# Projections of queries and keys multiplied into the convolutions' weights on chip

## The chip, the cores and the metric

The kernel runs on one core of one Trainium2 chip. The metric is the device time of one execution in microseconds. TensorE (PE), VectorE (DVE), ScalarE (ACT), GpSimd (POOL) and SyncE (SP, which here issues all DMAs) run their own instruction lists in order and meet at semaphores.

## What is computed

A decoder layer on x of 8 batches by 128 positions by 128 features, float32: attention with convolutions, attention over a context, and a mixture of experts, each on a normalised x and added to x. The change concerns the queries and keys of the first attention:

```python
q_in = linear(x, Wq_w, Wq_b).transpose(0, 2, 1)
Q3 = conv1d(q_in, convq_w, convq_b, (1, 1))
Q_cat = jnp.concatenate([q_in, Q3], axis=1).transpose(0, 2, 1)
Q = linear(Q_cat, qproj_w, qproj_b).reshape(b_, l_, H, DK).transpose(0, 2, 1, 3)
...
tau = sigmoid(conv1d(gelu(conv1d(x_conv, tau1_w, tau1_b, (1, 1), groups=D)), tau2_w, tau2_b, (0, 0)))
delta = sigmoid(conv1d(gelu(conv1d(x_conv, del1_w, del1_b, (1, 1), groups=D)), del2_w, del2_b, (0, 0)))
scores = jnp.einsum('bhqd,bhkd->bhqk', Q, K) / sqrt(DK)
scores = scores * tau[..., None] + delta[:, :, None, :]
```

Keys are made as queries are, with weights of their own. The convolutions have three taps and zero padding of one position at either end of each batch. H is 16, DK 8.

## The kernel before, in words

The features lie on the 128 partitions, the 1024 positions (8 batches of 128) along the free axis. A PSUM bank holds 512 float32 columns, so work goes in two halves c of four batches. Matrix products go through the helper `mm` (L473), so the profile gives nearly all of them line 474; they are told apart by their operands.

*Start.* SP loads x (L346), the first constants up to `kpb` (L348, semaphore `ld_f`), the rest of them (L349, `ld_a`), the context, `pack_b`, the mask and expert weights. VectorE makes the mean and variance, then the normalised `xn`, one batch at a time (L294). TensorE meanwhile folds the second projection into the convolution's three taps (L490 to L494: three 128x128 products for queries, three for keys, and a one-column product for each bias). VectorE copies the folds out of PSUM and adds the first projection to the middle tap (L1131 to L1136): `foldq`, `foldk`, `foldb`.

*Turned x.* TensorE turns the eight batches (L478), ScalarE copies each half into `xnT` (L875), which has a zero column at either end of each batch.

*Queries and keys.* TensorE multiplies `xnT` by `wqT` and `wkT` (L501 to L505, four 512-column products), ScalarE adds the biases and writes `qin` and `kin` (`biased`, L894), and TensorE runs three shifted products per half on these with the folded weights (L509 to L524).

*Taps.* The depthwise convolutions of tau and delta: ScalarE makes the first tap of each of four blocks (`first_tap`, L888), VectorE adds two more (`later_taps`, L1138), ScalarE takes gelu (L922, L926). TensorE sums tau's two blocks to one row per head (L516), ScalarE takes the sigmoid (L929), VectorE multiplies it onto the queries (`qc`, L1178).

*High and low parts.* Queries and keys are split into a float32r high part (ScalarE, `high_keys` L902, `high_queries` L933) and the remainder (VectorE, `low_keys` L1189, `low_queries` L1183). TensorE stacks them per group of heads with the selection matrices `pick` (L541 to L558), which waits for the high and low keys of both halves. ScalarE fills rows of the stacks with constants (L882), and SP copies these over for the second attention's keys (`get_maxima`, L376). SP then stores the split rows (L410 to L414) and loads the per-step key blocks (L427).

Then follow 16 steps of attention and 66 units of experts, which the change does not touch.

The order on every engine is written out by hand. PSUM banks: 2 and 3 hold the folds, 4 the folded biases, 0 and 1 the turned x, 5 and 6 the queries, 7 and 0 the keys, 3 and 4 tau.

Of the kernel before, what the change touches and what calls it, by code (L numbers as in the profile page):

```python
# [11 lines left out]
ALU = mybir.AluOpType  # L12
# [3 lines left out]
P = 128  # L16
B = 8
T = B * P
H, DK = 16, 8
G = 4  # L20
# [41 lines left out]
def decoder_layer(nc, x, ctxT, mask, pack_a, pack_b, w3, rowsd, outT):  # L62
# [3 lines left out]
    with ExitStack() as ctx:  # L66
# [32 lines left out]
        foldq = oT[:, 0:3, :]  # L99
# [30 lines left out]
        foldk = early[:, 0:3 * P].rearrange("p (k o) -> p k o", k=3)  # L130
# [59 lines left out]
        in_done = sem("in_done")  # L190
        in_copied = sem("in_copied")
# [277 lines left out]
        def _(pe):  # L469
# [20 lines left out]
            for n, (conv_w, proj, bias) in enumerate((("cq", "qp2T", "cqb"), ("ck", "kp2T", "ckb"))):  # L490
                for k in range(3):
                    c0 = cols_a[conv_w][0] + P * k
                    mm(bank[2 + n][:, P * k:P * k + P], pa[:, c0:c0 + P], A(proj))
                mm(bank[4][:, n:n + 1], A(proj), A(bias)).then_inc(folded, 1)  # L494
            for c in range(2):
                turn_inputs(0, c, bank[c])
            pe.wait_ge(ld_a, 16)
            pe.wait_ge(ld_ctx, 16)
            pe.wait_ge(ld_b, 16)
            pe.wait_ge(pads_ready, 6)  # L500
            for c in range(2):  # L501
                pe.wait_ge(xT_copied, c + 1)
                mm(bank[5 + c][:, :], A("wqT"), half(xnT, c)).then_inc(in_done, 1)
            for c in range(2):
                mm(bank[7 - 7 * c][:, :], A("wkT"), half(xnT, c)).then_inc(in_done, 1)  # L505

            pe.wait_ge(fold_copied, 4)
            pe.wait_ge(in_copied, 2)
            for c in range(2):  # L509
                for k in range(3):  # L510
                    last = mm(bank[5 + c][:, :], foldq[:, k, :], half(qin, c, k), k == 0, k == 2)
                last.then_inc(q_done, 1)

            pe.wait_ge(gelu_done, 2)
            pe.wait_ge(const_ready, 1)
            for c in range(2):  # L516
                for r in range(2):
                    last = mm(bank[3 + c][:, :], tau2r[:, r, :, :], conv[:, r, 4 * c:4 * c + 4, :], r == 0, r == 1)
                last.then_inc(tau_done, 1)
            pe.wait_ge(in_copied, 4)  # L520
            for c in range(2):
                for k in range(3):
                    last = mm(bank[7 - 7 * c][:, :], foldk[:, k, :], half(kin, c, k), k == 0, k == 2)
                last.then_inc(k_done, 1)  # L524

# [340 lines left out]
        def _(act):  # L866
# [10 lines left out]
            act.wait_ge(pads_ready, 6)  # L877
# [3 lines left out]
            for g in range(G):  # L881
                act.activation(kst[0][:, g, 4:B, :].rearrange("p b t -> p (b t)"),  # L882
                               xnT[:, 0, 0:1].broadcast_to([P, HALF]), ACT.Identity,
                               bias=key_rows[:, g:g + 1]).then_inc(kst_filled, 1)
            copy_inputs(0, 0, 0)
            copy_inputs(0, 1, 1)
# [6 lines left out]

            def biased(dst, n, bias, banks):  # L894

                for c in range(2):
                    act.wait_ge(in_done, 2 * n + c + 1)
                    act.activation(half(dst, c, 1), four(banks[c]), ACT.Identity, bias=A(bias)).then_inc(in_copied, 1)
# [16 lines left out]
            biased(qin, 0, "bq", (5, 6))  # L915
            first_tap(0, 1, "tau1", "tau1b")
            first_tap(1, 0, "del1", "del1b")
            biased(kin, 1, "bk", (7, 0))
            first_tap(1, 1, "del1", "del1b")
            for r in range(2):  # L920
                act.wait_ge(conv_done, r + 1)
                act.activation(conv[:, r, :, :], conv[:, r, :, :], ACT.Gelu).then_inc(gelu_done, 1)  # L922
            for r in range(2):
# [10 lines left out]

            act.wait_ge(k_done, 1)
            act.wait_ge(fold_copied, 4)
            high_keys(0, 0, 7, foldb[:, 1:2])
            high_queries(0)
            act.wait_ge(k_done, 2)
            high_keys(0, 1, 0, foldb[:, 1:2])  # L940
            high_queries(1)
# [164 lines left out]
        def _(dve):  # L1106
# [24 lines left out]
            for n, (dst, proj) in enumerate(((foldq, "qp1T"), (foldk, "kp1T"))):  # L1131
                dve.wait_ge(folded, n + 1)
                link(dve.tensor_copy(dst[:, :, :].rearrange("p k o -> p (k o)"), bank[2 + n][:, 0:3 * P]))
                dve.tensor_tensor(dst[:, 1, :], dst[:, 1, :], A(proj), ALU.add).then_inc(fold_copied, 1)
            for n, bias in enumerate(("qpb", "kpb")):
                dve.tensor_tensor(foldb[:, n:n + 1], bank[4][:, n:n + 1], A(bias), ALU.add).then_inc(fold_copied, 1)  # L1136
# [16 lines left out]
            for at in range(3):  # L1153
                for m in (Q_PARTS[at], 2 + K_PARTS[at]):
                    rows = pick[:, m, :, :].rearrange("p g r -> p (g r)").rearrange("p (h r) -> p h r", h=H)
                    dve.wait_ge(rows_ready, 3)
                    last = dve.tensor_copy(rows[:, :, S_MAX:32].rearrange("p h (d a) -> p h a d", a=3)[:, :, at, :],
                                           ident.rearrange("p (h d) -> p h d", h=H))
            last.then_inc(picks_ready, 1)
# [33 lines left out]
            dve.wait_ge(fold_copied, 4)  # L1193
# [648 lines left out]
```

## Time and profile before

| | us |
|---|---|
| median of 3 runs | 303.61 (303.39 to 304.05) |
| the profiled execution | 304.08 |
| its span, first to last instruction | 302.3 |
| PE busy | 284.5 (94%) |
| DVE busy | 228.2 (76%) |
| ACT busy | 192.6 (64%) |
| POOL busy | 184.0 (61%) |

TensorE is busy nearly all of the span, but busy shares are means over stages. A float32 matrix product is two MATMUL records with a weight load (LDWEIGHTS, PEld) each; one of float32r is a single record. Times within the trace count from the first instruction.

### The profile page before, as it was taken

How to read it: one execution, taken by the hardware profiler on the slowest of the kernel's cores; microseconds unless marked ns; L12 is line 12 of the kernel's file. 1: busy time of each engine (PE TensorE's matmuls, PEld its weight loads, DVE VectorE, ACT ScalarE, POOL GpSimd, SP SyncE). 2: the span in 40 equal slices, each digit the busy share in tenths (PEclk: the TensorE clock that was granted, in tenths of full speed). 3: DMA queues.
4: the chain of work that ended last, by engine and by line, in shares of the span. 5: the costliest groups of instructions: out<-in, count | busy, mean ns of one | idle time of the engine just before them, and what ended most of it. 6: DMA issues, size and time to landing. Idle time of an engine off the chain costs nothing.

```text
span 302.3 us, 5347 instructions
## 1 busy us (share of the span) xinstructions
PE 284.5 (94%) x1675; PEld 203.1 (67%) x1675; DVE 228.2 (76%) x512; ACT 192.6 (64%) x352; POOL 184.0 (61%) x262
## 2 busy tenths in 40 slices
PE   1999999999999999899889999999999999999994
PEld 1734576666655565456665788888888888888883
DVE  3896798799859886987896559789956676676664
ACT  2797747796884566456742797766655555555552
POOL 8240062097708870985177799999975665665661
PEclk9999989999999999999999999999999999999999
DMA  7920535457577243350000637666333353344321
GB/s 260 266 44 1 192 71 150 105 125 254 102 187 136 64 104 98 87 132 10 2 1 25 203 107 223 198 200 188 129 102 137 105 173 128 124 133 134 119 62 37
DMA packets 30636, 37.18 MB, mean 123 GB/s; under 512 B 5136, under 2 KB 19856, under 8 KB 30608
## 3 DMA queue, kind: packets, MB, share of 16 engines
q1 hardware_dynamic: 30608, 36.84, 42.2%
q8 instruction: 14, 0.23, 0.4%
q14 instruction: 14, 0.11, 0.1%
HBM read 28.43 MB, written 3.93 MB: 107 GB/s over the span
## 4 chain that ended last, share of the span: by engine, by line
PE 83%; DVE 9%; ACT 4%; DMA 2%; issue 2%; SPq 0%; ACTq 0%; DVEq 0%
PE bank L474 57%; PE bank L813 5%; PE bank L815 5%; PE bank L814 5%; PE bank L619 2%; PE bank L594 2%; PE bank L637 2%; DMA pa<-pack_a 2%; DVE rawmax L1214 2%; PE bank L606 1%; PE bank L480 1%; ACT conv L891 1%; PE bank L642 1%; PE bank L603 1%; ACT conv L922 1%
## 5 line engine op out<-in xcount | busy, mean ns | idle before, releaser
L1779 POOL TENSOR_TENSOR qbd<-vs,qbd 128x512 fp32r<-128x512 f32 x65 | 83.7, 1291 | 33.3 <-ACT qbd L1093 33.3
L474 PE MATMUL bank<-khl,stacks 128*128 128x512 f32 x396 | 101.4, 392 | 1.9 <-DVE vs L1575 1.9
L474 PEld LDWEIGHTS bank<-khl,stacks 128*128 128x128 f32 x396 | 73.6, 188 | 18.6 <-issue 3.7
L1606 DVE TENSOR_TENSOR conv<-bank,conv 128x512 f32<-128x512 f32 x60 | 41.5, 691 | 31.4 <-ACT bank L1057 28.3
L1057 ACT ACTIVATE bank<-bank 128x512 f32<-128x512 f32 x61 | 35.5, 582 | 43.9 <-PE bank L474 43.9
L1214 DVE TENSOR_REDUCE rawmax<-bank 128x4 f32<-128x512 f32 x64 | 43.3, 684 | 9.4 <-PE bank L474 8.4
L1093 ACT ACTIVATE qbd<-vs 128x512 fp32r<-128x512 f32 x65 | 40.6, 625 | 7.1 <-DVE vs L1583 4.6
L1614 DVE TENSOR_TENSOR vs<-conv,bank 128x512 f32<-128x512 f32 x61 | 41.9, 687 | 2.1
L474 PE MATMUL bank<-stacks 128*128 128x512 f32 x96 | 41.5, 482 | 1.1 <-DVE stacks L1524 0.6
L981 ACT ACTIVATE conv<-bank 128x512 f32<-128x512 f32 x64 | 35.1, 597 | 6.4 <-PE bank L474 5.6
L1743 POOL TENSOR_TENSOR stacks<-ring,stacks 128x384 fp32r<-128x384 f32 x33 | 33.7, 1021 | 1.4
L474 PE MATMUL bank<-qbd,stacks 128*128 128x512 f32 x64 | 30.3, 520 | 0.6 <-ACT conv L981 0.6
L990 ACT ACTIVATE qbd<-bank 32x512 fp32r<-32x512 f32 x40 | 23.4, 586 | 10.7 <-PE bank L606 10.4
L813 PE MATMUL bank<-qbd,stacks 128*128 128x512 f32 (+1 forms) x67 | 26.4, 394 | 0.7 <-POOL qbd L1779 0.6
L815 PE MATMUL bank<-qbd,stacks 128*128 128x512 f32 (+1 forms) x67 | 25.9, 387 | 0.0
L814 PE MATMUL bank<-qbd,stacks 128*128 128x512 f32 (+1 forms) x67 | 25.9, 386 | 0.0
L474 PE MATMUL bank<-conv,vs 128*9 128x128 f32 (+1 forms) x520 | 23.3, 279 | 0.3 <-ACT conv L922 0.3
L474 PEld LDWEIGHTS bank<-stacks 128*128 128x128 f32 x96 | 18.1, 194 | 6.4 <-issue 1.7
L969 ACT ACTIVATE oT<-bank 128x512 f32<-128x512 f32 x16 | 9.6, 597 | 15.2 <-PE bank L474 15.2
L1749 POOL CAST stacks<-ring 128x384 fp32r<-128x384 f32 x17 | 8.6, 504 | 17.2 <-ACT conv L981 9.5
L474 PEld LDWEIGHTS bank<-conv,vs 128*9 128x9 f32 (+1 forms) x520 | 12.4, 91 | 8.7 <-issue 5.7
L1230 DVE CAST qbd<-bank 32x512 fp32r<-32x512 f32 x24 | 16.7, 694 | 1.6 <-PE bank L606 1.0
(227 smaller groups left out, 431.6 us busy)
## 6 DMA issues: line engine op xcount, KB each, us to landing
conv<-coefficient_rows SPq DMA_DIRECT2D x122, 128.0 KB, 2.9
ring<-w SPq DMA_DIRECT2D x33, 192.0 KB, 3.6
stacks<-stacks SPq DMA_DIRECT2D x68, 64.0 KB, 2.1
split_rows<-stacks SPq DMA_DIRECT2D x6, 256.0 KB, 2.6
stacks<-split_rows SPq DMA_DIRECT2D x16, 96.0 KB
split_rows<-khl SPq DMA_DIRECT2D x3, 512.0 KB, 4.3
stacks<-split_rows SPq DMA_DIRECT2D x8, 192.0 KB
pa<-pack_a SPq DMA_DIRECT2D x1, 706.0 KB, 5.3
```

The costliest lines, as they stand in the source:

```text
L474: return pe.matmul(out, lhsT, rhs, start=start, stop=stop)
L813: pe.matmul(acc, whi(pair)[:, 2, :], hhi[:, w, cols], start=False, stop=False, skip_group_check=True)
L814: pe.matmul(acc, whi(pair)[:, 2, :], hlo[:, w, cols], start=False, stop=False, skip_group_check=True)
L815: pe.matmul(acc, wlo(pair)[:, 2, :], hhi[:, w, cols], start=False, stop=stop, skip_group_check=True).then_inc(down_done, 1)
L981: act.activation(probs[:, i % 8, :, :].rearrange("p j t -> p (j t)"), bank[2 + i % 2][:, :], ACT.Exp, scale=SCALE).then_inc(exped, 1)
L1057: act.activation(out, four(2 + p), ACT.Silu).then_inc(silu_done, 1)
L1093: act.activation(hhi[:, n % 4, :].rearrange("p (b t) -> p b t", b=4), hx[n % 4], ACT.Copy).then_inc(hhi_ready, 1)
L1214: dve.tensor_reduce(rawmax[:, s % 2, g, :].unsqueeze(2), bank[i % 2][:, :].rearrange("p (j k) -> p j k", j=J), AX.X, ALU.max, negate=True) ...
L1606: dve.tensor_tensor(out, gate, spread[:, n % ROWS, :, :], ALU.mult).then_inc(gate_scaled, 1)
L1614: dve.tensor_tensor(hx[n % 4], scaled[:, 4 * p:4 * p + 4, :], four(4 + p), ALU.mult).then_inc(h_done, 1)
L1743: pool.tensor_tensor(wlo(pair), ring[:, pair % RING, :, :], whi(pair).bitcast(F32), ALU.subtract).then_inc(wlo_ready, 1)
L1779: pool.tensor_tensor(hlo[:, n % 4, :].rearrange("p (b t) -> p b t", b=4), hx[n % 4], hhi[:, n % 4, :].bitcast(F32).rearrange("p (b t) -> p ...
```

## The change

The first projection (`wqT`, `wkT`) is multiplied on chip into the folded weights, so the convolutions run on `xnT` itself and `qin`, `kin` are no longer made; their memory now holds the folds and the two turned projection matrices.

- The middle tap gets the first projection by a product with the identity in PSUM (`fold`), no longer by an addition on VectorE. ScalarE copies the folds out.
- `wqT` and `wkT` are turned on TensorE and copied by ScalarE; `compose` multiplies one by its three folded taps, 384 columns in one product; ScalarE copies the result.
- The projections' biases enter the bias column by three one-column products on the folds (`sum_bias`). At a batch's first and last position one tap falls on padding, where the bias must not count: `convolve` takes it off there with two products of four columns by `negbias`.
- On TensorE, `turn_inputs` now stands behind `compose` and `sum_bias` of each half. The time scales of tau come between the two key halves.
- On ScalarE, one of the four key fills stays ahead of the turned x; the three others go between and behind the taps; the first tap of the last block follows tau's gelus; high queries come ahead of high keys.
- On VectorE, the selection matrices are made ahead of the taps; low queries come ahead of low keys.
- GpSimd's two large memsets wait for the normalised x instead of the folds; four small memsets of padding go.

```diff
-        foldq = oT[:, 0:3, :]
+        convq = oT[:, 0:3, :]
+        folds = [t[:, :, :].rearrange("p b t -> p (b t)")[:, 0:3 * P].rearrange("p (k o) -> p k o", k=3) for t in (qin, kin)]
+        natural = qin[:, :, :].rearrange("p b t -> p (b t)")[:, 4 * P:6 * P].rearrange("p (n i) -> p n i", n=2)
+        negbias = sb("negbias", [P, 2])
...
-        foldk = early[:, 0:3 * P].rearrange("p (k o) -> p k o", k=3)
+        convk = early[:, 0:3 * P].rearrange("p (k o) -> p k o", k=3)
...
@@ -487,42 +495,75 @@
 
             pe.wait_ge(ld_f, 16)
 
-            for n, (conv_w, proj, bias) in enumerate((("cq", "qp2T", "cqb"), ("ck", "kp2T", "ckb"))):
+            def fold(n, conv_w, proj, added):
+
                 for k in range(3):
                     c0 = cols_a[conv_w][0] + P * k
-                    mm(bank[2 + n][:, P * k:P * k + P], pa[:, c0:c0 + P], A(proj))
-                mm(bank[4][:, n:n + 1], A(proj), A(bias)).then_inc(folded, 1)
+                    last = mm(bank[2 + n][:, P * k:P * k + P], pa[:, c0:c0 + P], A(proj), True, k != 1)
+                    if k == 1:
+                        last = mm(bank[2 + n][:, P:2 * P], ident, A(added), False, True)
+                last.then_inc(folded, 1)
+
+            def compose(n):
+
+                pe.wait_ge(fold_copied, n + 1)
+                mm(bank[5 + n][:, 0:3 * P], natural[:, n, :], folds[n][:, :, :].rearrange("p k o -> p (k o)"))\
+                    .then_inc(composed, 1)
+
+            def sum_bias(n, proj, conv_bias, bias):
+
+                mm(bank[4][:, n:n + 1], A(proj), A(conv_bias), True, False)
+                for k in range(3):
+                    last = mm(bank[4][:, n:n + 1], folds[n][:, k, :], A(bias), False, k == 2)
+                last.then_inc(bias_summed, 1)
+
+            def convolve(n, weights, c, out):
+
+                for k in range(3):
+                    mm(out[:, :], weights[:, k, :], half(xnT, c, k), k == 0, k == 2)
+                edges = out[:, :].rearrange("p (b t) -> p b t", b=4)
+                for k, t in ((0, 0), (2, P - 1)):
+                    last = pe.matmul(edges[:, :, t:t + 1], folds[n][:, k, :],
+                                     negbias[:, n:n + 1].unsqueeze(2).broadcast_to([P, 4, 1]), start=False, stop=True,
+                                     skip_group_check=True)
+                return last
+
+            fold(0, "cq", "qp2T", "qp1T")
+            pe.wait_ge(ld_a, 16)
+            for n, w in enumerate(("wqT", "wkT")):
+                last = pe.transpose(bank[0][:, P * n:P * n + P], A(w), ident)
+            last.then_inc(natural_done, 1)
+            fold(1, "ck", "kp2T", "kp1T")
+            pe.wait_ge(natural_copied, 1)
+            compose(0)
+            sum_bias(0, "qp2T", "cqb", "bq")
+            turn_inputs(0, 0, bank[0])
+            compose(1)
+            sum_bias(1, "kp2T", "ckb", "bk")
+            turn_inputs(0, 1, bank[1])
+            pe.wait_ge(pads_ready, 2)
+            pe.wait_ge(bias_negated, 1)
             for c in range(2):
-                turn_inputs(0, c, bank[c])
-            pe.wait_ge(ld_a, 16)
+                pe.wait_ge(xT_copied, c + 1)
+                pe.wait_ge(compose_copied, c + 1)
+                convolve(0, convq, c, bank[5 + c]).then_inc(q_done, 1)
+
+            def time_scales():
+
+                pe.wait_ge(gelu_done, 2)
+                pe.wait_ge(const_ready, 1)
+                pe.wait_ge(bias_folded, 2)
+                for c in range(2):
+                    for r in range(2):
+                        last = mm(bank[3 + c][:, :], tau2r[:, r, :, :], conv[:, r, 4 * c:4 * c + 4, :], r == 0, r == 1)
+                    last.then_inc(tau_done, 1)
+
+            convolve(1, convk, 0, bank[7]).then_inc(k_done, 1)
+            time_scales()
+            convolve(1, convk, 1, bank[0]).then_inc(k_done, 1)
+
             pe.wait_ge(ld_ctx, 16)
             pe.wait_ge(ld_b, 16)
-            pe.wait_ge(pads_ready, 6)
-            for c in range(2):
-                pe.wait_ge(xT_copied, c + 1)
-                mm(bank[5 + c][:, :], A("wqT"), half(xnT, c)).then_inc(in_done, 1)
-            for c in range(2):
-                mm(bank[7 - 7 * c][:, :], A("wkT"), half(xnT, c)).then_inc(in_done, 1)
-
-            pe.wait_ge(fold_copied, 4)
-            pe.wait_ge(in_copied, 2)
-            for c in range(2):
-                for k in range(3):
-                    last = mm(bank[5 + c][:, :], foldq[:, k, :], half(qin, c, k), k == 0, k == 2)
-                last.then_inc(q_done, 1)
...
-            pe.wait_ge(in_copied, 4)
-            for c in range(2):
-                for k in range(3):
-                    last = mm(bank[7 - 7 * c][:, :], foldk[:, k, :], half(kin, c, k), k == 0, k == 2)
-                last.then_inc(k_done, 1)
...
-            for g in range(G):
+            def fill_keys(g):
+
                                bias=key_rows[:, g:g + 1]).then_inc(kst_filled, 1)
+
+            def copy_fold(n):
+
+                act.wait_ge(folded, n + 1)
+                act.activation(folds[n][:, :, :].rearrange("p k o -> p (k o)"), bank[2 + n][:, 0:3 * P], ACT.Copy)\
+                    .then_inc(fold_copied, 1)
+
+            def copy_composed(n, dst):
+
+                act.wait_ge(composed, n + 1)
+                act.activation(dst[:, :, :].rearrange("p k o -> p (k o)"), bank[5 + n][:, 0:3 * P], ACT.Copy)\
+                    .then_inc(compose_copied, 1)
+
+            fill_keys(0)
+            copy_fold(0)
+            act.wait_ge(natural_done, 1)
+            act.activation(natural[:, :, :].rearrange("p n i -> p (n i)"), bank[0][:, 0:2 * P], ACT.Copy)\
+                .then_inc(natural_copied, 1)
+            copy_fold(1)
+            copy_composed(0, convq)
             copy_inputs(0, 0, 0)
+            copy_composed(1, convk)
             copy_inputs(0, 1, 1)
...
-            def biased(dst, n, bias, banks):
-
-                for c in range(2):
-                    act.wait_ge(in_done, 2 * n + c + 1)
-                    act.activation(half(dst, c, 1), four(banks[c]), ACT.Identity, bias=A(bias)).then_inc(in_copied, 1)
...
             first_tap(0, 0, "tau1", "tau1b")
-            biased(qin, 0, "bq", (5, 6))
             first_tap(0, 1, "tau1", "tau1b")
+            fill_keys(1)
+            fill_keys(2)
             first_tap(1, 0, "del1", "del1b")
-            biased(kin, 1, "bk", (7, 0))
-            first_tap(1, 1, "del1", "del1b")
             for r in range(2):
                 act.wait_ge(conv_done, r + 1)
                 act.activation(conv[:, r, :, :], conv[:, r, :, :], ACT.Gelu).then_inc(gelu_done, 1)
+            first_tap(1, 1, "del1", "del1b")
+            fill_keys(3)
             for r in range(2):
                 act.wait_ge(conv_done, 3 + r)
...
+            act.wait_ge(bias_folded, 2)
+            high_queries(0)
+            high_queries(1)
             act.wait_ge(k_done, 1)
-            act.wait_ge(fold_copied, 4)
             high_keys(0, 0, 7, foldb[:, 1:2])
-            high_queries(0)
             act.wait_ge(k_done, 2)
             high_keys(0, 1, 0, foldb[:, 1:2])
-            high_queries(1)
...
-            for n, (dst, proj) in enumerate(((foldq, "qp1T"), (foldk, "kp1T"))):
-                dve.wait_ge(folded, n + 1)
-                link(dve.tensor_copy(dst[:, :, :].rearrange("p k o -> p (k o)"), bank[2 + n][:, 0:3 * P]))
-                dve.tensor_tensor(dst[:, 1, :], dst[:, 1, :], A(proj), ALU.add).then_inc(fold_copied, 1)
+            dve.wait_ge(ld_a, 16)
+            for n, bias in enumerate(("bq", "bk")):
+                last = dve.tensor_scalar(negbias[:, n:n + 1], A(bias), -1.0, None, ALU.mult)
+            last.then_inc(bias_negated, 1)
+            for at in range(3):
+                for m in (Q_PARTS[at], 2 + K_PARTS[at]):
+                    rows = pick[:, m, :, :].rearrange("p g r -> p (g r)").rearrange("p (h r) -> p h r", h=H)
+                    dve.wait_ge(rows_ready, 2)
+                    last = dve.tensor_copy(rows[:, :, S_MAX:32].rearrange("p h (d a) -> p h a d", a=3)[:, :, at, :],
+                                           ident.rearrange("p (h d) -> p h d", h=H))
+            last.then_inc(picks_ready, 1)
+            dve.wait_ge(bias_summed, 2)
             for n, bias in enumerate(("qpb", "kpb")):
-                dve.tensor_tensor(foldb[:, n:n + 1], bank[4][:, n:n + 1], A(bias), ALU.add).then_inc(fold_copied, 1)
+                dve.tensor_tensor(foldb[:, n:n + 1], bank[4][:, n:n + 1], A(bias), ALU.add).then_inc(bias_folded, 1)
...
-            for at in range(3):
-                for m in (Q_PARTS[at], 2 + K_PARTS[at]):
-                    rows = pick[:, m, :, :].rearrange("p g r -> p (g r)").rearrange("p (h r) -> p h r", h=H)
-                    dve.wait_ge(rows_ready, 3)
-                    last = dve.tensor_copy(rows[:, :, S_MAX:32].rearrange("p h (d a) -> p h a d", a=3)[:, :, at, :],
-                                           ident.rearrange("p (h d) -> p h d", h=H))
-            last.then_inc(picks_ready, 1)
...
-            dve.wait_ge(fold_copied, 4)
+            low_queries(0, 0)
             low_keys(0, 0, 7, foldb[:, 1:2])
-            low_queries(0, 0)
+            low_queries(0, 1)
             low_keys(0, 1, 0, foldb[:, 1:2])
-            low_queries(0, 1)
...
-            pool.wait_ge(fold_copied, 4)
+            pool.wait_ge(xn_ready, B)
             pool.memset(qbd[:, :, :, :, :].bitcast(F32), 0.0).then_inc(rows_ready, 1)
```

## Rows read from the trace of the kernel before

**Rows 1.** The chain that ended last, first 40 us: start, length, what.
```profile
1.22 5.34 DMA pa<-pack_a
12.29 3.21 PE bank L474 x4
22.70 14.12 PE bank L474 x38
36.84 1.29 DVE stacks L1202 x2
```

**Rows 2.** Timeline of TensorE's products: start, length, line, operation, output<-inputs, shape, count, idle before.
```profile
6.61 3.58 PE L474 MATMUL bank<-pa 128*128 128x128 f32 x16 [6.61 <-DMA pa<-pack_a]
10.05 2.25 PE L480 MATMUL bank<-pa,xn 128*128 128x128 f32 x8
22.70 3.70 PE L474 MATMUL bank<-conv,vs 128*128 128x512 f32 x8 [0.34 <-ACT conv L922]
26.23 5.31 PE L474 MATMUL bank<-kin,vs 128*128 128x512 f32 x12
31.38 1.88 PE L474 MATMUL bank<-ctxs,pb 128*128 128x512 f32 x4
33.20 4.19 PE L474 MATMUL bank<-stacks 128*128 128x512 f32 x16
```

**Rows 3.** Timeline of TensorE's weight loads, and four turns of a later stage.
```profile
13.89 0.34 PEld L474 LDWEIGHTS bank<-xnT,pa 128*128 128x128 f32 x1 [0.52 <-issue]
14.74 0.34 PEld L474 LDWEIGHTS bank<-xnT,pa 128*128 128x128 f32 x1 [0.52 <-issue]
38.02 0.97 PEld L474 LDWEIGHTS bank<-pa,conv 128*128 128x128 f32 x8
43.43 2.04 PEld L474 LDWEIGHTS bank<-pa,xnT 128*128 128x128 f32 x8
52.19 0.64 PE L637 MATMUL bank<-pa,oT 128*128 128x128 f32 x4
```

**Rows 4.** Stretches: length, busy time of PE, PEld, DVE, ACT, POOL, granted clock, DMA share, GB/s.
```profile
14.00:15.00 1.00, 1.00 (x3) 0.48 (x2) 0.49 (x1) 0.94 (x2) 1.00 (x1) 1.00 0.50 70
42.30:45.80 3.50, 3.35 (x13) 2.77 (x12) 3.24 (x11) 2.05 (x5) 2.78 (x1) 0.51 0.31 63
```

**Rows 5.** Timeline of ScalarE.
```profile
7.26 2.55 ACT L882 ACTIVATE stacks<-xnT,key_rows 128x512 fp32r<-128x512 f32 x4 [5.05 <-DVE key_rows L1127]
12.33 0.60 ACT L875 ACTIVATE xnT<-bank 128x512 f32<-128x512 f32 x1 [0.43 <-PE bank L480]
13.13 1.23 ACT L891 ACTIVATE conv<-xnT,pa 128x1024 f32<-128x1024 f32 x1
25.05 0.63 ACT L926 ACTIVATE conv<-conv 128x512 f32<-128x512 f32 x1 [1.36 <-DVE conv L1145]
27.51 1.26 ACT L929 ACTIVATE tauT<-bank,pa 128x512 f32<-128x512 f32 x2
29.59 0.62 ACT L933 ACTIVATE stacks<-qc 128x512 fp32r<-128x512 f32 x1
```

**Rows 6.** Timeline of VectorE.
```profile
9.62 2.14 DVE L294 TENSOR_SCALAR xn<-xres,mv,nwt 128x128 f32<-128x128 f32 x8
14.51 1.28 DVE L1143 SCALAR_TENSOR_TENSOR conv<-xnT,pa,conv 128x1024 f32<-128x1024 f32 x1 [1.03 <-ACT conv L891]
23.73 1.28 DVE L1145 SCALAR_TENSOR_TENSOR conv<-xnT,pa,conv 128x1024 f32<-128x1024 f32 x1
24.93 0.93 DVE L1157 CAST stacks<-pa 128x128 fp32r<-128x128 f32 x6
28.72 1.41 DVE L1178 SCALAR_TENSOR_TENSOR qc<-bank,foldb,tauT 128x512 f32<-128x512 f32 x2 [2.62 <-ACT tauT L929]
32.30 0.75 DVE L1189 SCALAR_TENSOR_TENSOR stacks<-bank,foldb,stacks 128x512 fp32r<-128x512 f32 x1 [0.92 <-ACT stacks L902]
```

**Rows 7.** SP's issue of the copied maxima.
```profile
9.84 7.26 SPq L379 DMA_DIRECT2D stacks<-stacks  x8
```

More of the change, by code:

```diff
@@ L189, in decoder_layer @@
         fold_copied = sem("fold_copied")
-        in_done = sem("in_done")
-        in_copied = sem("in_copied")
+        natural_done = sem("natural_done")
+        natural_copied = sem("natural_copied")
+        composed = sem("composed")
+        compose_copied = sem("compose_copied")
+        bias_summed = sem("bias_summed")
+        bias_folded = sem("bias_folded")
+        bias_negated = sem("bias_negated")
         v_done = sem("v_done")
@@ L507, in _ @@
-            pe.wait_ge(fold_copied, 4)
-            pe.wait_ge(in_copied, 2)
-            for c in range(2):
-                for k in range(3):
-                    last = mm(bank[5 + c][:, :], foldq[:, k, :], half(qin, c, k), k == 0, k == 2)
-                last.then_inc(q_done, 1)
-            pe.wait_ge(gelu_done, 2)
-            pe.wait_ge(const_ready, 1)
-            for c in range(2):
-                for r in range(2):
-                    last = mm(bank[3 + c][:, :], tau2r[:, r, :, :], conv[:, r, 4 * c:4 * c + 4, :], r == 0, r == 1)
-                last.then_inc(tau_done, 1)
@@ L875, in copy_inputs @@
                 act.activation(half(xnT, c, 1), four(b), ACT.Copy).then_inc(xT_copied, 1)
-            act.wait_ge(pads_ready, 6)
+            act.wait_ge(pads_ready, 2)
             act.activation(warm[:, :], xnT[:, 0, 0:1], ACT.Gelu).then_inc(warmed, 1)
             act.wait_ge(keys_ready, 1)
-            for g in range(G):
+            def fill_keys(g):
                 act.activation(kst[0][:, g, 4:B, :].rearrange("p b t -> p (b t)"),
@@ L892, in first_tap @@
                                bias=pa[:, b0:b0 + 1], scale=pa[:, w0:w0 + 1]).then_inc(conv_part, 1)
-            def biased(dst, n, bias, banks):
-                for c in range(2):
-                    act.wait_ge(in_done, 2 * n + c + 1)
-                    act.activation(half(dst, c, 1), four(banks[c]), ACT.Identity, bias=A(bias)).then_inc(in_copied, 1)
             def high_keys(n, c, b, bias):
@@ L1684, in _ @@
         def _(pool):
-            for t in (xnT, qin, kin):
-                pool.memset(t[:, :, 0:1], 0.0).then_inc(pads_ready, 1)
-                pool.memset(t[:, :, P + 1:P + 2], 0.0).then_inc(pads_ready, 1)
+            pool.memset(xnT[:, :, 0:1], 0.0).then_inc(pads_ready, 1)
+            pool.memset(xnT[:, :, P + 1:P + 2], 0.0).then_inc(pads_ready, 1)
             pool.memset(kbd[:, :, :, :, :].bitcast(F32), 0.0).then_inc(rows_ready, 1)
```

## The prediction

> **What bounds the kernel now.** I read the page first, then the chain that ended last, then the timeline of one engine at a time over the first 46 us, since every edited line runs there. The chain [rows 1] shows what to look for: the constants' DMA until 6.57, TensorE's folds and turns, TensorE again at 12.29, then ScalarE (a strip left out here) until a stretch of TensorE alone from 22.70 to 36.81, and only then VectorE's stacking. From 33.20 on (the stacks, [rows 2]) nothing is edited but the time at which it starts. So the question is one number: when do the stacking products at 33.20 start in the new kernel? A delay there is a delay of the whole, since behind it every engine's work hangs on those stacks and the later part is bound by TensorE.
>
> Two chains meet at 33.20. The first is TensorE's own: 12 records of the key convolution and 4 of the second keys, 26.23 to 33.1 without a gap [rows 2]. The second is that of the depthwise taps: the turned x is in SBUF at 12.93, the first tap starts at 13.13 on ScalarE [rows 5], VectorE's eight later taps run from 14.51 to 25.01 with 0.27 us between them in all [rows 6], Gelu of the last tap starts at 25.05, the sigmoids run 27.51 to 28.77 [rows 5], qc starts 28.72, and the last low half of the keys, 32.30 to 33.05, starts behind 0.92 us of idle [rows 6]. The reader is to see how little slack that second chain has: 0.92 us. Whatever the change takes off TensorE is worth at most that until the taps become the bound; whatever it adds before 12.93 is paid in full soon after.
>
> **TensorE's two speeds.** The granted clock is shown as 1.00 for 14 to 15 us [rows 4], yet weight loads of the 512-column products start 0.85 us apart there (13.89, 14.74) [rows 3], while 12 such records take 5.31 us, 0.43 each, from 26.23 [rows 2]. I go by the spacing: 1.2 GHz until about 15, then 2.4. From 42.30 to 45.80 the granted clock is 0.51 [rows 4], the low level again. Small records have both prices too: at the low level 0.215 (16 records from 6.61 to the turns' start at 10.05, [rows 2]) or 0.255 (8 loads in 2.04, [rows 3]); at the high one 0.12 (8 loads in 0.97, with 16 columns behind each, [rows 3]). A float32 product is two records. This matters because the change puts new small products into the low stretch.
>
> **What the change adds before x is turned.** TensorE is in order. Before, the 16 records of the folds end at 10.05 and the eight turns keep up with VectorE's xn, 9.62 to 11.76 [rows 6], ending at 12.30 [rows 2]. Now, from 6.61:
> - fold of queries, 4 products, 8 records by 0.215: 8.3. Turning wqT and wkT, two records, about 0.2 each: 8.7. Its wait for the second constants is met, since they are issued before 2.3 and TensorE reaches it past 8.3. Fold of keys, 8 records: 10.5. ScalarE's four key fills took 2.55 us, 0.64 each [rows 5]; now only one precedes the copies of fold and turned weights, which end near 9.4, under the second fold.
> - compose(0), 384 columns: 2 x 0.75 x 0.85 = 1.28 us low, 0.64 high. sum_bias(0), 4 one-column products, 8 records: 1.75 low, 0.97 high. The first four turns: 0.85 low, 0.5 high (four turns as one row took 0.64 with its tail, [rows 3]). Then compose(1), sum_bias(1), the other four turns, the same again. Three of each four one-column products are new, as are both compositions.
> - all low: 10.5 + 2 x (1.28 + 1.75 + 0.85) = 18.3. All high from 10.5: 10.5 + 2 x 2.11 = 14.7. High from the end of compose(0) at 11.8: 11.8 + 0.97 + 0.5 + 2.11 = 15.4. I take the last: from 6.6 to 11.8 TensorE now streams 128- and 384-column products with 0.4 us of turns inside; in the kernel before, 3.4 us of folds followed by paced turns left it low, and 512-column products without a gap, from 12.09, raised it near 15.
> - the last x copy takes 0.6 behind it: 16.0 in place of 12.93, a shift of 3.1 us (bounds 2.4 and 6.0).
>
> The Trainium skill ("TensorE: Matmul & The Clock Gate", LDWEIGHTS) has a weight load take its columns divided by 1.2 GHz, whatever the array's level. At 128 columns that is 0.107 us, and an estimate by it would cut the all-low case by some 1.7 us. The rows speak against it: 8 small loads took 0.97 us high and 2.04 low [rows 3].
>
> **What it removes, and why that does not pay.** Four 512-column products (8 records, 0.85 or 0.43 each) and four biased copies on ScalarE go. The copies lay between the first taps and pushed the gelus of tau. Without them tau's gelus are ready 20.8 + 3.1 = 23.9. TensorE: each convolution half is 6 records by 0.43 and 4 edge records by 0.12 = 3.06. Three halves from 15.4 end at 24.6, time scales (8 records, from 22.70 to 26.23 with the wait, 3.43 by 0.43) 28.0, the last half 31.1, second keys (4 records) 1.7: 32.8 [rows 2]. A return to the low level for 3.4 us would make it 34.5. The edge records have no row of their own; between 0.12 and 0.43 each the 16 of the four halves cost at most 5 us more, 37.8 as the worst end; I take 0.12, the row of other small products.
>
> The tap chain, shifted: VectorE needs its 10.5 us less the 0.27 gap, so the taps end 24.75 + 3.1; gelus, table load and sigmoids keep their steps, qc ends at 29.87 + 3.1. Then the new ScalarE order runs two high queries (0.62 each) and two high keys (as a sigmoid of the same shape, 0.63 apart) one behind another [rows 5], the last ending at 31.9 + 3.1 and VectorE's fourth low half at 33.4 + 3.1 = 36.5. In the kernel before, the high key of half 0 was done while qc ran. The 0.93 us of picks [rows 6] moved ahead of the taps costs nothing either way: it lay in 2.62 us of idle, and now lies in VectorE's wait for x. Bias sums likewise.
>
> So the stacks start at 36.5 in place of 33.2: **+3.3 us**, set by the taps; TensorE (32.8) is hidden with 3.7 us in hand, so that the products removed gain nothing.
>
> Moved DMAs: SP's eight copies of the maxima, 7.26 us of issue from 9.84 [rows 7], now wait for the fourth key fill, behind the last first tap: about 22.5 + 3.1 = 25.6 to 32.9. Behind them on SP's queue are the row stores, which wait for the low keys at 36.5 anyway: nothing lost, 3.6 us in hand. POOL's large memsets no longer wait for the folds; they end earlier.
>
> The sum: profiled execution 304.08 (span 302.3 and 1.78 around it) + 3.3 = 307.4; the median of the three runs lies 0.47 below the profiled one, so 306.9.
>
> **Rivals.**
> - *The level stays low until the convolutions*: x copied 18.9, shift 6.0, stacks at 39.4: +6.2, 309.8. For it: in the kernel before, it stayed low through 3.4 us of the same folds, and the sparse stretch ahead of 42.30 dropped it again; compositions are short, and what lies between them is sparse. Against: the dense stretch is now 5 us. The Trainium skill, same page (PE-mode transpose), says that transposes do not count as busy for the gate; by it the turns help no more than a pause, which would make this rival likelier. 0.21.
> - *Small products hide behind each other*, only their columns counting: 10.5 + 2 x (0.64 + 0.5) and 0.2 for the sums = 13.0, x copied 13.6, +0.9: 304.5. Against it, 0.12 per record even where only 16 columns stream. 0.07.
> - *TensorE's stream sets the end, the taps don't* (the other side): if the tail from sigmoid to low keys runs concurrently enough to end by 33.2, the place that decides is TensorE's end: 32.8 at my shift, 32.1 at the smallest: -0.4 to -1.1, about 302.8. For it, the chain names TensorE alone from 22.70 to 36.81; against it, the idle of only 0.92 us at 32.30. It would need the tap chain 3.3 us shorter than worked out. 0.06.
> - *The low stretch at 42.30 does not come back*: up to half of its 3.4 us, -1.7, on top of the forecast: 305.2. 0.08. It lies within slower.
>
> **The numbers.** Forecast +3.3 with 0.58. Faster than 303.0 needs the third rival: 0.06. Within 0.2% of before (0.6 us, about what a measurement of this kernel can tell from no change) takes pieces of the second and third: 0.05. Slower: 0.89. The range goes from the hidden-small-products case, 304.5, to the low-level case with a little above it, 310.1.
>
> **What would show it.** Right: the last xT copy near 16, first tap near 16.2, taps to about 28, sigmoids near 30.5, the first stacking product near 36.5 and a gap on TensorE ahead of it; the chain through ScalarE and VectorE taps instead of TensorE from 22.7. Loads of the bias sums 0.12 apart past 11.8 show the level, 0.22 the first rival. Wrong: x copied before 14, or stacks that start ahead of 34, or a chain through TensorE's convolutions and edges.

## The result, and the profile after

The changed kernel takes 308.12 us (median of 4 runs, 307.90 to 308.68), the kernel before 303.83 in the same comparison: a ratio of 1.0141, 95% interval 1.0122 to 1.0159. That is 4.3 us slower where 3.3 were forecast; the time lies 1.2 us above the forecast of 306.9 and inside its range. The profiled execution takes 307.90 with a span of 306.1, against 304.08 and 302.3: +3.8.

TensorE, VectorE and ScalarE are busy for 284.9, 226.8 and 192.7 us, each within 1.4 us of before. The busy times say nothing here; the place does. The chain that ended last, of the kernel after (start, length, what), from the last turn of x to the stacks:

```profile
13.57 0.51 PE bank L488 x4
14.11 0.60 ACT xnT L916
...
15.01 1.14 ACT conv L954
...
16.29 1.30 DVE conv L1209
...
25.16 1.30 DVE conv L1211
26.48 0.63 ACT conv L984
...
27.64 1.28 ACT L987
28.94 0.70 ACT tauT L987
...
30.71 0.76 DVE qc L1237
...
32.73 0.75 DVE stacks L1248
...
34.00 0.75 DVE stacks L1248
34.76 0.14 issue
34.89 5.90 PE bank L482 x14
```

Where [rows 1] had TensorE alone from 22.70 to 36.81, the chain now goes through ScalarE's first tap, VectorE's eight taps without a gap, gelu, sigmoid and the split of keys and queries. TensorE's products of the kernel after:

```profile
6.59 2.08 PE L482 MATMUL bank<-pa 128*128 128x128 f32 x8 [6.59 <-DMA pa<-pack_a]
8.88 1.33 PE L482 MATMUL bank<-pa 128*128 128x128 f32 x8
10.05 0.81 PE L482 MATMUL bank<-qin 128*128 128x384 f32 x2
...
16.48 0.50 PE L526 MATMUL bank<-negbias,qin 128*128 128x4 f32 x4
...
22.89 3.68 PE L482 MATMUL bank<-conv,vs 128*128 128x512 f32 x8
...
29.34 1.96 PE L482 MATMUL bank<-ctxs,pb 128*128 128x512 f32 x4
34.89 6.35 PE L482 MATMUL bank<-stacks 128*128 128x512 f32 x16 [3.58 <-DVE stacks L1248]
```

Two things are to be seen. The second keys end at 31.3 and the stacks start at 34.89, behind 3.58 us of idle; in [rows 2] they start at 33.20 behind none. And the same 16 records take 6.35 us where they took 4.19. The stretches of the kernel after (columns as in [rows 4]) show why:

```profile
31.30:34.80 3.50, 0.01 (x1) 0.00 (x0) 2.83 (x6) 2.94 (x5) 0.00 (x0) 0.79 0.35 50
34.80:40.10 5.30, 5.21 (x12) 4.13 (x13) 1.86 (x3) 2.06 (x3) 0.00 (x0) 0.50 0.80 297
40.10:46.90 6.80, 5.98 (x36) 4.56 (x34) 6.07 (x14) 3.43 (x5) 2.38 (x1) 1.00 0.20 39
46.90:50.40 3.50, 3.50 (x13) 3.12 (x14) 3.44 (x11) 2.37 (x5) 3.12 (x2) 0.51 0.57 126
```

While TensorE stands idle its granted clock drops, some 2 us into the gap: it is 0.84 in the mean of 33.0 to 33.5 and 0.50 from 33.5 on. The stacks run at 0.50, the 1.2 GHz level, until they are nearly done. The last row is the low stretch that [rows 4] has at 42.30; it is there in this kernel too. So the 3.8 us of the span are 34.89 - 33.20 = 1.7 us of a later start and 6.35 - 4.19 = 2.2 us of slower stacks. That is arithmetic on two traces; the experiments test both terms.

### The profile page after: what moved, and what is told of

Read it like the earlier page. It is cut to its first block, busy times and chain, and to the rows that moved or that the text cites. A ratio compares the mean times of both kernels' runs of the same rounds, so it can differ in the third digit from the quotient of the medians.

```text
span 306.1 us, 5403 instructions
## 1 busy us (share of the span) xinstructions
PE 284.9 (93%) x1705; PEld 206.8 (68%) x1705; DVE 226.8 (74%) x510; ACT 192.7 (63%) x353; POOL 184.7 (60%) x258
## 4 chain that ended last, share of the span: by engine, by line
PE 78%; DVE 13%; ACT 3%; issue 2%; DMA 2%; SPq 0%; ACTq 0%; DVEq 0%
PE bank L482 53%; PE bank L854 5%; PE bank L856 5%; PE bank L855 5%; PE bank L660 2%; PE bank L635 2%; PE bank L678 2%; DVE rawmax L1272 2%; DMA pa<-pack_a 2%; DVE conv L1211 2%; DVE conv L1209 2%; PE bank L647 1%; PE bank L683 1%; PE bank L644 1%; PE bank L488 1%
## 5 line engine op out<-in xcount | busy, mean ns | idle before, releaser
L1836 POOL TENSOR_TENSOR qbd<-vs,qbd 128x512 fp32r<-128x512 f32 x65 | 83.7, 1289 | 33.4 <-ACT qbd L1151 33.3
L1664 DVE TENSOR_TENSOR conv<-bank,conv 128x512 f32<-128x512 f32 x60 | 41.5, 691 | 31.5 <-ACT bank L1115 28.3
L482 PE MATMUL bank<-stacks 128*128 128x512 f32 x96 | 43.7, 510 | 4.8 <-DVE stacks L1248 3.6
L482 PEld LDWEIGHTS bank<-stacks 128*128 128x128 f32 x96 | 20.1, 213 | 10.5 <-issue 5.9
L854 PE MATMUL bank<-qbd,stacks 128*128 128x512 f32 (+1 forms) x67 | 26.4, 394 | 0.7 <-POOL qbd L1836 0.6
L1027 ACT ACTIVATE oT<-bank 128x512 f32<-128x512 f32 x16 | 9.6, 598 | 15.2 <-PE bank L482 15.2
L322 POOL TENSOR_TENSOR xres<-xres,pa 128x1024 f32<-128x1024 f32 x1 | 2.4, 2377 | 25.2 <-issue 25.2
```

The costliest lines, as they stand in the source:

```text
L482: return pe.matmul(out, lhsT, rhs, start=start, stop=stop)
L854: pe.matmul(acc, whi(pair)[:, 2, :], hhi[:, w, cols], start=False, stop=False, skip_group_check=True)
L1664: dve.tensor_tensor(out, gate, spread[:, n % ROWS, :, :], ALU.mult).then_inc(gate_scaled, 1)
L1836: pool.tensor_tensor(hlo[:, n % 4, :].rearrange("p (b t) -> p b t", b=4), hx[n % 4], hhi[:, n % 4, :].bitcast(F32).rearrange("p (b t) -> p ...
```

## The experiments

Each ran beside the kernel before on the same chip (303.51 us for the four with the dead products in the idle time, x turned early, the delayed stacks and both edits; 303.85 for the other four; 303.83 beside the first row of the changed kernel). Between these groups, compare the distances to the kernel before, not the times. "Stacks" is the start of the first stacking product and the length of the row of 16, in each profile; the last column is the span less that start.

| kernel | time, us | ratio to before (95%) | stacks: start, length | rest of span |
|---|---|---|---|---|
| before | 303.51; 303.85 | 1 | 33.20, 4.19 | 269.1 |
| changed | 308.12 | 1.0141 (1.0122 to 1.0159) | 34.89, 6.35 | 271.2 |
| changed, again | 308.64 | 1.0161 (1.0139 to 1.0182) | 36.29, 5.46 | 270.2 |
| dead products in the idle time | 306.10 | 1.0091 (1.0056 to 1.0126) | 35.78, 4.18 | 268.9 |
| x turned early | 305.01 | 1.0052 (1.0026 to 1.0078) | 33.57, 4.20 | 268.7 |
| before, stacks delayed | 307.76 | 1.0130 (1.0091 to 1.0169) | 36.01, 5.50 | 270.8 |
| keys split first | 304.63 | 1.0019 (1.0006 to 1.0033) | 34.25, 4.20 | 268.9 |
| both of these | 302.96 | 0.9975 (0.9956 to 0.9995) | 32.37, 4.24 | 268.8 |
| both, and dead products at the start | 302.40 | 0.9955 (0.9938 to 0.9972) | 31.82, 4.19 | 268.9 |
| before, dead products at the start | 303.65 | 0.9998 (0.9982 to 1.0014) | 33.40, 4.18 | 269.4 |

The last two columns hold most of the case. Behind the start of the stacks every kernel needs 268.7 to 269.4 us, except the three in which the stacks' row is over 5 us long.

**Dead products in the idle time.** The changed kernel and, ahead of the waits for the stacks:

```diff
+            pe.wait_ge(tau_ready, 2)
+            for i in range(4):
+                mm(bank[3][:, :], ident, ctxs[:, 4 * (i % 2):4 * (i % 2) + 4, :])
             pe.wait_ge(picks_ready, 1)
```

> The changed kernel with four dead 512-column float32 products by the identity into bank 3 between the second keys and the stacks, where TensorE stood idle from 31.3 to 34.9 us. Theory (the idle time drops TensorE to its low level, and the stacks then run 5.9 us instead of 3.6): the stacks still start near 34.9, take 3.6 us, and the time falls by some 2.3 us, to 305.8. Rival (the stacks are slow because ScalarE's and VectorE's copies of them, or SP's row stores beside them, take longer): no change, 308.1, or a little more.

TensorE's rows in it:

```profile
32.03 3.60 PE L482 MATMUL bank<-ctxs,pa 128*128 128x512 f32 x8
35.78 4.18 PE L482 MATMUL bank<-stacks 128*128 128x512 f32 x16
```

and the stretch of the stacks:

```profile
35.70:39.80 4.10, 4.02 (x16) 2.96 (x17) 2.38 (x4) 2.71 (x5) 0.00 (x0) 1.00 0.81 301
```

Work that computes nothing makes the kernel 1.7 to 2.2 us faster: +2.6 over before, against +4.3 and +4.8 for the changed kernel in its two comparisons. The time came near the 305.8 expected, but the start did not: it is 35.78, not 34.9. The last copy of x ended at 15.6 in this profile, 0.9 us later than in the first, and the start moved by as much. The row of the stacks takes 4.18 us, as in the kernel before. The stacks run at the full clock with the same copies beside them (2.38 and 2.71 us of VectorE and ScalarE) and a DMA share of 0.81. The rival falls.

**Before, stacks delayed.** The kernel before with, ahead of its low keys on VectorE:

```diff
+            for i in range(6):
+                link(dve.tensor_tensor(oT[:, :, :], half(tauT, 0), half(tauT, 0), ALU.add))
             low_keys(0, 0, 7, foldb[:, 1:2])
```

> The kernel before with six dead additions of 128x512 on VectorE (about 0.73 us each, chained) between qc and the low keys, so that the stacks start some 3.5 us later and TensorE stands idle for as long behind the second keys. Theory: the idle time drops TensorE to the low level here too, and the stacks take 5.9 instead of 3.6 us: 3.5 + 2.3 = +5.8, 309.6. Rival (idle time costs only itself): +3.5, 307.3.

Measured +4.25 us, or 307.76: nearer to the rival's 307.3 than to 309.6, so the time alone does not decide between them. The profile does, for the execution that it shows. The start moved by 2.8 us, not 3.5: the level rose earlier in this run than in the profile before (the projections took 3.67 us, not 5.12), so that the whole start ran ahead, VectorE's qc from 28.19 instead of 28.72 and TensorE's second keys until 32.4 instead of 33.3. TensorE's products and the stretch at the stacks:

```profile
30.50 1.88 PE L474 MATMUL bank<-ctxs,pb 128*128 128x512 f32 x4
36.01 5.50 PE L474 MATMUL bank<-stacks 128*128 128x512 f32 x16 [3.64 <-DVE stacks L1189]
```
```profile
36.00:39.10 3.10, 3.09 (x7) 2.47 (x8) 1.28 (x3) 1.38 (x2) 0.00 (x0) 0.50 0.76 281
```

The old kernel, none of whose products changed, pays a toll too in this execution, behind 3.64 us of idle: 1.3 us in the stacks on top of the 2.8. The second size was expected too large as well: the low level covered 3.1 us of the stacks here, not all of them. TensorE's wait of 0.66 us for SP's key blocks, ahead of 46.41, is part of the rest. The four runs lie in two pairs: 308.27 and 308.53 with a mean clock of 0.989 and 0.987 (the profiled one), 306.88 and 307.24 with 0.993, near the 0.994 of profiles that hold a single low stretch. The pairs are 1.3 us apart, as much as the toll in the profile. This suggests, and no profile shows, that the stacks of the faster pair ran at the high level behind the same idle time.

**The changed kernel again.** No edit.

> The changed kernel as it is, on the same chip as the next three, as their anchor. Theory: +4.3 over the kernel before, stacks near 34.9 behind 3.6 us of idle TensorE, the granted clock near 0.5 in them. Where a run should show the high level in them, the time should be 2 us lower.

This profile shows how much hangs on when the level rises. Composition and stacks on TensorE, the last copy of x on ScalarE, and the stretch of the stacks:

```profile
10.87 1.38 PE L482 MATMUL bank<-qin 128*128 128x384 f32 x2
...
36.29 5.46 PE L482 MATMUL bank<-stacks 128*128 128x512 f32 x16 [3.59 <-DVE stacks L1248]
```
```profile
15.49 0.60 ACT L916 ACTIVATE xnT<-bank 128x512 f32<-128x512 f32 x1 [0.79 <-PE bank L488]
```
```profile
36.20:39.30 3.10, 3.01 (x7) 2.46 (x8) 0.68 (x2) 1.38 (x2) 0.00 (x0) 0.50 0.74 271
```

The first composition took 1.38 us, low, where the first profile had 0.81 at 10.05, high already. x was copied at 16.1 here and at 14.7 there, the stacks started at 36.29 and 34.89. The start moved by 3.1 us over before and the stacks lost 1.3; in the first profile it was 1.7 and 2.2. What differs in the stacks is how much of them the low level covers, 5.3 us there and 3.1 here. Either way some 4 us.

**x turned early.** Both halves turned right behind the first composition, ScalarE's copies in that order, the bias column finished after tau's taps:

```diff
             compose(0)
-            sum_bias(0, "qp2T", "cqb", "bq")
             turn_inputs(0, 0, bank[0])
-            compose(1)
-            sum_bias(1, "kp2T", "ckb", "bk")
             turn_inputs(0, 1, bank[1])
+            compose(1)
+            sum_bias(0, "qp2T", "cqb", "bq")
+            sum_bias(1, "kp2T", "ckb", "bk")
```

> The changed kernel with both halves of x turned right behind the first composition, ahead of the second one and of the bias sums; the bias column is finished after tau's taps. Theory (the late turn costs 1.8 us through the tap chain): x copied near 12.9 instead of 14.7, stacks at 33.1 instead of 34.9; 306.3 if the low level at the stacks comes all the same behind a shorter idle of 1.8 us, 304.0 if it does not. Rival (TensorE's own stream, with its edge products, would set the start of the stacks as soon as the taps are earlier): they start no earlier than its end at 31.3, so this rival forbids nothing here, but the stacks would then start at 31.3 and the time be near 302.5.

```profile
29.78 1.96 PE L482 MATMUL bank<-ctxs,pb 128*128 128x512 f32 x4
33.57 4.20 PE L482 MATMUL bank<-stacks 128*128 128x512 f32 x16 [1.83 <-DVE stacks L1247]
```

These rows of TensorE give an idle time of 1.83 us and stacks at full speed. The start is 33.57, where 33.1 was expected. ScalarE's rows say why:

```profile
11.64 1.09 ACT L916 ACTIVATE xnT<-bank 128x512 f32<-128x512 f32 x2
12.76 0.49 ACT L937 ACTIVATE vs<-bank 128x384 f32<-128x384 f32 x1
13.14 0.41 ACT L968 ACTIVATE vs<-pa 128x256 f32<-128x256 f32 x1
13.45 2.36 ACT L954 ACTIVATE conv<-xnT,pa 128x1024 f32<-128x1024 f32 x2
```

x is copied at 12.7, 2.0 us earlier than in the first profile, but the copy of the second composition (L937) now lies between x and the first tap, which starts only 1.45 us earlier (13.45 for 14.90); 1.3 us of it reach the stacks. Its ten runs lie in two groups: four of 306.15 to 306.49 with a mean clock of 0.989, the six others of 304.16 to 305.37 with 0.993 to 1.000. Both ends that were expected occur. The late turn costs what the tap chain passes on. The profile is of one of the faster six; for the slower four, the toll is read from their times and clocks alone. By these, a shorter idle time makes the toll rarer: all eight runs of the changed kernel have a mean clock of 0.983 to 0.989, four of the ten here have 0.989. TensorE's stream did not set the start.

**Keys split first.** ScalarE makes the high part of key half 0 while it waits for the last tap, VectorE its low part behind the taps; half 1 comes between the two halves of the queries:

```diff
             for r in range(2):
+                if r == 1:
+                    act.wait_ge(bias_folded, 2)
+                    act.wait_ge(k_done, 1)
+                    high_keys(0, 0, 7, foldb[:, 1:2])
                 act.wait_ge(conv_done, 3 + r)
...
-            act.wait_ge(bias_folded, 2)
             high_queries(0)
-            high_queries(1)
-            act.wait_ge(k_done, 1)
-            high_keys(0, 0, 7, foldb[:, 1:2])
             act.wait_ge(k_done, 2)
             high_keys(0, 1, 0, foldb[:, 1:2])
+            high_queries(1)
...
+            low_keys(0, 0, 7, foldb[:, 1:2])
+
             def values(n, c, bias, b0):
...
             low_queries(0, 0)
-            low_keys(0, 0, 7, foldb[:, 1:2])
+            low_keys(0, 1, 0, foldb[:, 1:2])
             low_queries(0, 1)
-            low_keys(0, 1, 0, foldb[:, 1:2])
```

> The changed kernel with x still turned late, and only the keys split ahead of the queries. Theory (the tail behind the sigmoids is the other half of the idle time): stacks near 32.8 instead of 34.9, idle 1.5 us, the low level mostly gone: 304.0 (306.0 with it). Rival (only the late turn matters): stacks at 34.5 or later, 307.5.

```profile
34.25 4.20 PE L482 MATMUL bank<-stacks 128*128 128x512 f32 x16 [1.37 <-DVE stacks L1227]
```

Alone it takes the kernel from +4.8 to +0.8 us on the same chip. Expected were 304.0 and a start at 32.8, counted from the first profile's 34.9; against the profile of the same chip, with its start at 36.29, the start is 2.0 us earlier, as much as was expected. Of the four operations that VectorE had between qc and the stacks two are left, and the idle time of 1.37 us (this row is TensorE's) drops nothing: all twelve runs have a mean clock of 0.992 or more. Here x was turned as late as in the changed kernel, its last copy ending at 16.3.

**Both.** The two edits together.

> As the one with x turned early, and the keys split ahead of the queries: high and low part of key half 0 while the last taps run, of half 1 between the two high queries. Theory (the tail behind the sigmoids is what held the stacks, TensorE's stream comes next): stacks near 31.3, at the end of the second keys, no idle of TensorE ahead of them, no low level there: 303.8 - 1.9 = 301.9. Rival (the tail is set by the queries alone, sigmoid to low query): stacks no earlier than 32.8, 303.4, or 305.5 with the low level.

```profile
30.57 1.96 PE L482 MATMUL bank<-ctxs,pb 128*128 128x512 f32 x4
32.37 4.24 PE L482 MATMUL bank<-stacks 128*128 128x512 f32 x16
```

TensorE runs through without a gap, and its own stream sets the start, 1.1 us later than expected, since the level rose later than in the first profile: its first composition took 1.40 us, not 0.81. VectorE's last low key was ready at 32.23, so the two chains end almost together. 302.96 us are 1.1 more than the 301.9 expected and 0.55 less than the kernel before takes.

**Both, with dead products at the start.** Three products of 512 columns on zeros ahead of the wait for the constants (VectorE clears them first), and, unlike in the version with both edits, the first bias sums ahead of the turns. Of the diff, the dead products:

```diff
+            pe.wait_ge(zeros_ready, 1)
+            for i in range(3):
+                mm(bank[7][:, :], conv[:, 0, 0, :], conv[:, 0, 0:4, :])
             pe.wait_ge(ld_f, 16)
```

> x turned early, keys split first, and three dead 512-column products on zeros while TensorE waits for the constants before 6.6 us, so that the folds meet the high level. Theory: folds' records 0.12 instead of 0.215, TensorE's stream ends near 30.8 instead of 32.4, stacks near 31.5, set by low query and low key: 302.1 against 302.96 without the dead products. Rival (x, not TensorE, sets the convolutions, or the level falls again before them): no change, 303.0.

```profile
1.44 5.48 PE L483 MATMUL bank<-conv 128*128 128x512 f32 x6 [1.44 <-DVE conv L1182]
6.71 1.12 PE L483 MATMUL bank<-pa 128*128 128x128 f32 x8
...
28.95 1.96 PE L483 MATMUL bank<-ctxs,pb 128*128 128x512 f32 x4
31.82 4.19 PE L483 MATMUL bank<-stacks 128*128 128x512 f32 x16 [0.91 <-DVE stacks L1231]
```

Eight fold records in 1.12 us instead of 2.08, stacks at 31.82 where 31.5 was worked out. Now VectorE sets the start, behind 0.91 us of idle on TensorE. This version is faster than the kernel before and the changed one: 302.40 us, 1.45 below before. Against the version with both edits the gain is less sure: it ran on another chip, it has one more difference of order, and the intervals of the two ratios overlap (0.9938 to 0.9972 and 0.9956 to 0.9995).

**Before, with dead products at the start.** The same products in the kernel before.

> The kernel before with the same three dead products ahead of the constants. Theory (its projections ran at the low level until 15 us, and TensorE's stream set the stacks): the projections take 3.4 instead of 5.1 us, but the stacks gain at most the 0.92 us of idle that VectorE had ahead of them: 303.5 - 0.8 = 302.7. Rival (ScalarE's biased copies and taps set it alone): 303.5.

```profile
6.88 1.95 PE L475 MATMUL bank<-pa 128*128 128x128 f32 x16 [0.85 <-DMA pa<-pack_a]
10.24 2.26 PE L481 MATMUL bank<-pa,xn 128*128 128x128 f32 x8 [1.42 <-DVE xn L295]
12.30 5.10 PE L475 MATMUL bank<-xnT,pa 128*128 128x512 f32 x8
```
```profile
5.10:8.90 3.80, 2.87 (x19) 1.96 (x17) 3.53 (x25) 1.41 (x3) 1.89 (x12) 1.00 1.01 405
...
12.00:15.20 3.20, 3.20 (x6) 1.62 (x6) 2.10 (x7) 2.60 (x4) 1.45 (x1) 0.50 0.69 163
```

No difference of the medians that can be measured (0.9982 to 1.0014). In the profile TensorE waits 0.85 us between the dead products and the constants. The folds are faster, so it then waits 1.42 us for x and turns it at VectorE's pace; the clock drops again (0.50 for 12.0 to 15.2), and the projections take 5.10 us as in the kernel before. In the profile of the version before this one, where the work behind the dead products is dense, the level held. The profile alone does not decide whether the projections' low level costs the kernel before anything, since they ran low in it. The twelve runs say more: six took 303.89 to 304.80 with a mean clock of 0.987 to 0.991 (the profiled one, 304.53, is among them), the six others 303.04 to 303.42 with 0.992 to 1.000. Two of these six have a clock of 1.000, which leaves no room for a fall like that at 12.0. So the level may hold in some executions, which are then up to 0.8 us faster than the kernel before, as the theory had it, and be lost in others. It is a hint only: no profile shows a faster one, and the kernel before itself ranges from 302.95 to 304.66 on that chip.

## Why the prediction was right, and where it was not

- *A fixed number of microseconds behind the start of the stacks.* Right: 268.7 to 269.4 in all kernels with fast stacks.
- *x turned later, taps shifted, all of it paid.* Right in mechanism, though not in full. x was copied at 14.7 and, in the other profile, 16.1; forecast 16.0, bounds 15.3 and 18.9, so the first lies 0.6 below the lower bound. The term "all high from 10.5" assumed that the folds were low: in the first profile the second fold already took 1.33 us for its 8 records, against 1.91 in the second profile. The taps ended at 26.4, and 8.45 us later came the stacks; 8.65 were worked out. Not all of the later start is the turn's: the taps end 1.4 us later than before (26.4 for 25.0), and VectorE had 0.92 us of idle [rows 6] to absorb this, so that with the old order of keys and queries an estimate from these rows gives +0.5 us. The rest of the 1.7 comes from the new order, which puts all four high and low parts behind qc. The prediction had this tail in its sum of 8.65 us, but put the whole +3.3 down to the taps. The experiments agree: splitting keys first brings the start 2.0 us forward, turning early 1.3.
- *TensorE's products removed gain nothing.* Right: its stream ended at 31.3 (first profile) and waited. Four edge records took 0.36 us (16.48 to the next product at 16.84), 0.09 each; 0.12 was assumed.
- *"TensorE (32.8) is hidden with 3.7 us in hand."* This is the step that failed, though the total came out inside the range. The idle time was counted as free. It was there, 3.58 us, and it dropped the clock under the stacks, which start the serial part: 2.2 us in one profile, 1.3 in the other. The prediction had read the low stretch behind sparse work [rows 4] and did not apply it to a gap that it had itself worked out. The Trainium skill ("TensorE: Matmul & The Clock Gate", Why this matters for your kernels) advises against idle gaps between bursts of matmuls for this reason; the traces agree, by 4.19 against 6.35 us in the same 16 records, the latter behind 3.58 us of idle.
- *The total.* In the first profile -1.6 us on the start (34.9 for 36.5) and +2.2 on the stacks cancel in part: that the time came nearer than the terms is luck. In the profile of the second comparison the start (36.29) was near the forecast, and the toll of 1.3 us stands on top of it.
- *Rival "the low level until the convolutions"*: did not occur in any profile of the changed kernel; but the level's rise moved from run to run. *"Small products hide"*: no, the turns started 0.81 us after the 8 bias records (10.70 to 11.51), 0.10 us each where 0.12 was assumed. *"TensorE's stream sets the end"*: not in the changed kernel; in the one with both edits, it does.
- *"The low stretch at 42.30 does not come back"* was priced at up to 1.7 us. It came back (0.51 for 46.90 to 50.40), and it was mis-sized: the kernel with x turned early had no low stretch there in its profile and needed 268.7 us behind its stacks, against 269.1 for the kernel before. The kernel before has it in some runs and not in others: its runs with a mean clock of 0.999 or more average 303.7 us, those with 0.994 or less 303.9, on either chip. It is worth about 0.2 us. That VectorE's maxima pace that part is likely from the chain, but not tested.
- *Moved DMAs*: the maxima went out from 24.27 to 31.54, ahead of the row stores at 34.84. They are not on the chain that ended last, as forecast.

## What to carry to other kernels

Products taken off an engine gain nothing if another chain ends later, and work put ahead of that chain's first link costs all but the slack that the chain has: order the feeding engine by what the slow chain needs first, and look at the order of the small operations at the chain's end, which here cost as much. An idle stretch of TensorE ahead of a serial stage is not free time in hand: price the work behind it at both clock levels. Dead products in the gap gave 1.7 to 2.2 us back; removing the cause of the gap, here an order of small operations, gave 4.0. Dead products at the start kept the level up in the profile in which dense work followed and lost it in the one with a wait of 1.42 us and paced turns behind; look at the mean clock of every run, not of the profiled one only.

## What the runs showed that was not expected

- Two profiles of the same kernel differ by 1.4 us in when x is copied (14.7 and 16.1) and by 0.9 us in the stacks (6.35 and 5.46), in opposite senses; they differ by 0.4 us of span. Read one alone, and each gives another cause the larger share.
- Idle stretches of 3.6 us ahead of the stacks came with the low level in three profiles of three; of 1.83, 1.37 and 0.91 us in none of three profiles, though the run times and clocks of the first of these suggest that it happens in four runs of ten. Those of the kernel before with its stacks delayed suggest that even 3.6 us do not always bring it.
- The granted clock is shown as 1.00 ahead of its first rise too, where only the spacing of the records tells the level. In the kernel with both edits and dead products at the start it is 1.00 for 3.0 to 4.8, while weight loads of the dead 512-column products start at 2.45, 3.30 and 4.16, some 0.85 us apart; at the high level they are 0.43 apart.
